# A four-layer graph network on one core: the last-but-one attention layer gathers normed rows and multiplies them by the weights tile by tile

## The reference, cut to what matters

```
h = jnp.maximum(_layernorm(x, axis=-1), 0.0)
x = x + _L2_gnn_ref(h, edge_index, L2_gnn_weight, L2_gnn_attn_l, L2_gnn_attn_r)

xt = jnp.matmul(x, weight).reshape(-1, heads, out_ch)      # heads 4, out_ch 64
row, col = (edge_index[0], edge_index[1])
alpha_l = jnp.einsum('ehd,hd->eh', xt[row], attn_l)
alpha_r = jnp.einsum('ehd,hd->eh', xt[col], attn_r)
alpha = jax.nn.softmax(jax.nn.leaky_relu(alpha_l + alpha_r, 0.01), axis=1)
tmp = jnp.einsum('nh,nhd->nd', alpha[:n], xt[col[:n]])
out = jnp.broadcast_to(tmp[:, None, :], (n, heads, out_ch))
```

## Time and profile before

| | us |
|---|---|
| median of 3 runs | 3559.73 |
| lowest, highest run | 3539.03, 3561.72 |
| the profiled execution, its time | 3567.03 |
| its span | 3565.2 |
| PE busy | 2424.9 (68%) |
| DVE busy | 2395.4 (67%) |
| POOL busy | 1734.6 (49%) |
| ACT busy | 1352.5 (38%) |

### The profile page before, as it was taken

How to read it: one execution, slowest core, us unless ns; L and a number is a source line. 1 busy time by engine, 2 the same in 40 slices (tenths; PEclk the granted TensorE clock), 3 DMA queues, 4 the chain that set the end, 5 groups by cost and what they waited for, 6 DMA issues and landing times. The chain is left out here.

```text
span 3565.2 us, 41686 instructions
## 1 busy us (share of the span) xinstructions
PE 2424.9 (68%) x12339; PEld 1976.6 (55%) x12339; DVE 2395.4 (67%) x4693; ACT 1352.5 (38%) x2800; POOL 1734.6 (49%) x1269
## 2 busy tenths in 40 slices
PE   4668733454555543666621999879999999925998
PEld 3522213454444443444421897469888988923788
DVE  5979945777777778877886544344565566615788
ACT  2268833444444441000000435424434434423776
POOL 0257887776667667888888777730000000042000
PEclk9779865555555555888855999889999999966999
DMA  9993224665555656555533774146545645340355
GB/s 373 351 355 34 22 26 130 174 171 164 165 165 166 172 170 137 133 142 134 143 40 39 202 177 89 1 103 185 175 126 172 185 130 173 118 103 8 109 173 176
DMA packets 338453, 517.84 MB, mean 145 GB/s; under 512 B 145379, under 2 KB 227100, under 8 KB 331580
## 3 DMA queue, kind: packets, MB, share of 16 engines
q1 hardware_dynamic: 190254, 436.41, 38.2%
q0 software_dynamic: 134768, 58.41, 14.2%
q10 hardware_dynamic: 13214, 20.35, 1.7%
HBM read 369.65 MB, written 145.38 MB: 144 GB/s over the span
## 5 line engine op out<-in xcount | busy, mean ns | idle before, releaser
L1133 PE MATMUL banks<-rows_r,lhs_r 128*128 128x448 f32 x3500 | 899.1, 372 | 84.0 <-issue 41.6
L728 POOL DMA_INDIRECT counts<-wts x391 | 637.4, 1630 | 307.9 <-DMA counts<-ring 141.0
L1133 PEld LDWEIGHTS banks<-rows_r,lhs_r 128*128 128x128 f32 x3500 | 667.8, 191 | 152.9 <-issue 74.8
L741 POOL DMA_INDIRECT weights<-wts x391 | 620.9, 1588 | 161.8 <-issue 159.1
L1133 PE MATMUL banks<-ring_r,lhs_r 128*128 128x448 f32 x1750 | 525.8, 370 | 0.0
L749 POOL DMA_INDIRECT reg<-tab_p,w x416 | 406.9, 978 | 217.9 <-issue 122.8
L548 DVE SCALAR_TENSOR_TENSOR ring_r<-ring,dinv,rows_r 128x896 fp32r<-128x896 f32 (+1 forms) x300 | 303.7, 1033 | 309.5 <-ACT rows_r L535 309.3
L1221 PE MATMUL banks<-lhs_r,oT 128*128 x416 | 203.3, 489 | 429.8 <-issue 346.6
L535 ACT ACTIVATE rows_r<-ring,dinv 128x896 fp32r<-128x896 f32 (+1 forms) x300 | 285.0, 951 | 399.3 <-PE banks L1133 342.0
L799 POOL DMA_INDIRECT el<-tab_l,base_i x25 | 24.0, 958 | 796.8 <-DMA tab_l<-reg 789.5
L1221 PEld LDWEIGHTS banks<-lhs_r,oT 128*128 128x128 f32 x416 | 131.9, 317 | 447.3 <-issue 447.0
(11 more groups left out here) (269 smaller groups left out, 4104.6 us busy)
## 6 DMA issues: line engine op xcount, KB each, us to landing
ring<-weights SPq DMA_DIRECT2D x225, 448.0 KB
ring<-counts SPq DMA_DIRECT2D x150, 448.0 KB
zbuf<-reg SPq DMA_DIRECT2D x208, 256.0 KB
reg<-zbuf SPq DMA_DIRECT2D x52, 1024.0 KB
counts<-ring SPq DMA_DIRECT2D x25, 1568.0 KB, 16.4
weights<-ring SPq DMA_DIRECT2D x25, 1568.0 KB
ring<-weights SPq DMA_DIRECT2D x75, 224.0 KB
dr<-low_rows_d SPq DMA_DIRECT2D x52, 256.0 KB
```

Source lines behind the costliest of these rows:

```text
L728: pool.indirect_dma_start(counts, bass.IndirectOffsetOnAxis(ap=ix_c[:, k:k + 1], axis=0), vals_c[:, k:k + 1], None, compute_op=ALU.add).th ...
L741: pool.indirect_dma_start(weights, bass.IndirectOffsetOnAxis(ap=ix_w[:, k:k + 1], axis=0), vals_w[:, k:k + 1], None, compute_op=ALU.add).t ...
L1133: m = pe.matmul(bank[:, 0:BLK], lhs[part], rows[:, c:c + BLK], start=first, stop=last)
```

## The change

Four things are changed.

1. The table `tab_x` holds the normed rows themselves (256 columns of `g_nat`) and no longer their product. SP stores a step as soon as ACT has written it.
2. PE no longer multiplies all 25 node tiles by 264 columns. It transposes them (`gT2`), and then makes only the left logits, 4 columns for each tile, all in one bank (stage `lg`); ACT copies them with one instruction and SP stores `tab_l`.
3. POOL issues the gathers of rows for steps 0 and 1 first, then waits for `tab_l`, and then alternates: left logits of step s-1, rows of step s+1.
4. When the rows of a step have landed, PE transposes each gathered tile (stage `gx`), ACT copies it to one of two buffers `edge_T`, PE multiplies it by 260 columns (stage `xt`), and ACT copies the product to `xt_edge`. ACT does these ten copies (`copy_rows(q)`) ahead of the exponential of the step, and `logits(q)` on DVE waits for the last of them.

The core of the diff:

```
+def rows_step(q):
+    ts = range(q * LG, (q + 1) * LG)
+    order = [(ts[0], "gx")]
+    for t in ts[1:]:
+        order += [(t, "gx"), (t - 1, "xt")]
+    return order + [(ts[-1], "xt")]
+
+def normed_groups(q):
+    return range(max(0, q - 2) * LG // 4 if q > 1 else 0, -(-NT // 4) if q == NSPLIT else max(0, q - 1) * LG // 4)
...
     # SP
             for s in range(NSPLIT):
-                sp.wait_ge(drained_a, nth[number["xt", ((s + 1) * LG - 1,)]])
-                if s == NSPLIT - 1:
-                    sp.dma_start(tab_l.rearrange("(t p) c -> p t c", p=P), xt_nat[:, :, XE:XW]).then_inc(l_stored, 16)
+                sp.wait_ge(ln_out, 2 * NT + (s + 1) * LG)
                 sp.dma_start(tab_x[s * LG * P:(s + 1) * LG * P].rearrange("(t p) c -> p t c", p=P),
-                             xt_nat[:, s * LG:(s + 1) * LG, 0:XE]).then_inc(xt_stored, 16)
+                             g_nat[:, s * LG:(s + 1) * LG, :]).then_inc(xt_stored, 16)
+            sp.wait_ge(drained_a, nth[number["lg", (0,)]])
+            sp.dma_start(tab_l.rearrange("(t p) c -> p t c", p=P), lg_nat).then_inc(l_stored, 16)
...
     # POOL
-            pool.wait_ge(l_stored, 16)
-            for s in range(NSPLIT):
-                for t in range(s * LG, (s + 1) * LG):
+            pool.wait_ge(xt_stored, 16 * NSPLIT)
+            for s in range(NSPLIT + 1):
+                for t in range(s * LG, (s + 1) * LG) if s < NSPLIT else ():
+                    pool.indirect_dma_start(x_edge[:, t, :], None, tab_x, ...).then_inc(edge_x[s], 16)
+                if s == 1:
+                    pool.wait_ge(l_stored, 16)
+                for t in range((s - 1) * LG, s * LG) if s else ():
                     pool.indirect_dma_start(el[:, t, :], None, tab_l, ...)
-                if s == 0:
-                    pool.wait_ge(xt_stored, 16 * NSPLIT)
-                for t in range(s * LG, (s + 1) * LG):
-                    pool.indirect_dma_start(xt_edge[:, t, :], None, tab_x, ...)
...
     # ACT
-            def copy_rows(g):
-                for t in tiles_of((g,), 4):
-                    bank = empty_bank(act, number["xt", (t,)])
-                    emptied(act.activation(xt_nat[:, t, :], bank[:, 0:XW], ACT.Copy))
+            def copy_rows(q):
+                for t, stage in rows_step(q):
+                    bank = empty_bank(act, number[stage, (t,)])
+                    if stage == "gx":
+                        emptied(act.activation(edge_T[t % 2], bank[:, 0:H], ACT.Copy))
+                    else:
+                        emptied(act.activation(xt_edge[:, t, :], bank[:, 0:XE], ACT.Copy))
...
             def exponentials(q):
+                copy_rows(q)
                 act.wait_ge(exp_in, q + 1)
...
     # PE
-            to_T("gT2", g_nat, ln_out, 2 * NT, behind=row_group)
-            to_T("gT3", g_nat, ln_out, 3 * NT)
+            to_T("gT2", g_nat, ln_out, 2 * NT)
+            bank = open_bank(number["lg", (0,)])
+            pe.wait_ge(drained_a, nth[number["gT2", (JH - 1, 6)]])
+            for t in range(NT):
+                for k in range(JH):
+                    m = pe.matmul(bank[:, t * HEADS:(t + 1) * HEADS], gT2[:, k, t * P:(t + 1) * P], gatw[:, k, XE:XW], ...)
+            m.then_inc(filled, 1)
+            def edge_rows(q):
+                pe.wait_ge(edge_x[q], 16 * LG)
+                for t, stage in rows_step(q):
+                    ...
+                    if stage == "xt":
+                        pe.wait_ge(drained_a, nth[number["gx", (t,)]])
+                    for k in range(JH):
+                        if stage == "gx":
+                            m = pe.transpose(bank[:, k * P:(k + 1) * P], x_edge[:, t, k * P:(k + 1) * P], ident[:, :])
+                        else:
+                            m = pe.matmul(bank[:, 0:XE], edge_T[t % 2][:, k * P:(k + 1) * P], gatw[:, k, 0:XE], ...)
+            for q in range(NSPLIT + 1):
+                if q < NSPLIT:
+                    edge_rows(q)
+                to_T("gT3", g_nat, ln_out, 3 * NT, groups=normed_groups(q))
...
     # DVE, logits(q)
-                v.wait_ge(edge_x[q], 16 * LG)
+                v.wait_ge(drained_a, nth[number["xt", ((q + 1) * LG - 1,)]])
```

48 lines of the change are left out of this document (21 added, 27 removed).

## The result

| | before | after |
|---|---|---|
| median, us | 3558.68 | 3594.48 |
| lowest, highest of 4 runs | 3539.03, 3561.72 | 3591.11, 3600.09 |
| the profiled execution's span | 3565.2 | 3589.3 |
| stage, first product of the node products to the fourth layer's products | 170.8 | 203.4 |
| ahead of the stage | 3094.4 | 3082.5 |

What follows compares the result with a forecast made beforehand. The third layer's stage, up to the fourth layer's products, was taken as the bound. Step 4 later by 5.4 us plus 10 for late hand-overs made +15 on 3559.7, stated as 3574; range 3546 to 3594, 8 in 10.

Steps and rivals of the forecast that it cites:

- narrow products: On PE ahead of the logits' store: 100 passes of 4 columns take 10 us, between 9 and 18.
- late hand-overs: Delayed dependent instructions on DVE beside POOL's gathers, steps 0 to 2: 10 us added, between 0 and 24.
- step 0: DVE's first step in the third layer's stage: begins at 3162 us, 8 us sooner, held by the logits.
- T: Ten ACT copies and the products between them, on the path in four steps: 9.4 us each, break-even 8.1.
- tail: From the start of step 4 to the fourth layer's products: same instructions, unchanged at 22.7 us.
- first row gather: POOL's first gather of rows in the stage: near 3131.3 us, against 3159.59 before.
- T of 11.0: Copies and products of a step with PE at half clock throughout: 11.0 us, making the time 3581.
- lock between VectorE and GpSimd: Shared SBUF port: only two-input DVE instructions late, by one gather of 0.96 us; set aside for the trace rows.
- The sum: Whole kernel: +5.4 for the start of step 4 and +10 for hand-overs, +15 on the median 3559.7.
- C: Rival, DVE's steps 0 and 1: hand-overs late through all gathers, +24 in place of +10, 3589; chance 0.22.
- B: Rival, a small gain: PE bursts warm or nearly so, or no hand-over late, 3551; chance 0.28.
- Past 1% only with T = 11.0 too: Claim on the slower rival: it passes 3595 only if T is also 11.0, adding 6.4; slower by over 1%, 0.08.

Runs made afterwards that it cites:

- both: Changed kernel with each step's ten copies made one step ahead and the 4-column products made group by group between transposes: 3455.42 us, ratio 0.9993 to the kernel before.
- lg_one_tile: Changed kernel with the 4-column products, and ACT's copy of the logits, cut to one of the 25 node tiles: 3602.21 us.
- ring_late_before: Kernel before, with SP issuing the six ring loads only after the last gather has landed: ratio 0.9994 to the kernel before.

## Why the prediction was wrong, point by point

Two terms of the sum failed. The narrow products were put at 10 us and took 21.5, and the late hand-overs were put at 10 us and took 25.7; the first moved the start of step 0, the second stretched step 1. The fourfold T, the main mechanism of the forecast, was right. That the median falls only half a microsecond outside the range is luck in part, since two smaller terms, T and the tail, were off the other way by 7.9 us together.

The forecast's places are put on before's clock, so after's times have 11.84 us added (3094.35 - 3082.51).

**The first row gather: right.** Forecast 3131.3. POOL's first, its wait for the logits, and its last gather:

```profile
3119.21 1.03 POOL L814 DMA_INDIRECT reg<-tab_x,tot  x1 [769.76 <-DMA tab_x<-reg]
...
3148.72 0.95 POOL L819 DMA_INDIRECT el<-tab_l,base_i  x1 [17.10 <-DMA tab_l<-reg]
...
3198.05 0.95 POOL L819 DMA_INDIRECT el<-tab_l,base_i  x1 [0.30 <-issue]
```

3119.21 + 11.84 = 3131.05. The pitch of a gather is 1.26 us, forecast 1.29.

**The narrow products: wrong, 10 forecast, 21.5 measured**, and outside the bounds of 9 and 18. Two errors are in that term. The clock: I took full clock "as PE has been at full clock for 29 us", but in those 29 us its list held the wide products that the change removes. After:

```profile
3107.00:3112.00 5.00, 3.52 (x17) 2.50 (x16) 1.28 (x11) 5.00 (x12) 0.00 (x0) 0.71 0.39 131
3112.00:3118.00 6.00, 4.20 (x15) 2.60 (x14) 0.00 (x0) 6.00 (x14) 0.00 (x0) 0.50 0.64 218
3118.00:3140.00 22.00, 21.51 (x101) 21.54 (x102) 0.00 (x0) 0.35 (x4) 9.68 (x10) 0.50 0.43 60
```

PE had only transposes beside layer norm 2, waited between them, and stood at half clock when the 50 products began, and through all of them. The price: I scaled by a row of 50 columns, 0.18 us at half clock, as an upper bound. The passes took 0.215, and PEld is busy for 21.54 of the 22 us. The 0.18 was misread: the start of the first of four pipelined products is not a full pitch ahead of the second. The weight loads of the same four products, in the trace before, are evenly spaced:

```profile
601.52 0.97 PEld L1230 LDWEIGHTS banks<-ring,reg 128*128 128x128 f32 x4
602.37 0.33 PEld L1221 LDWEIGHTS banks<-lhs_r,oT 128*128 128x128 f32 x1
```

They are (602.37 - 601.52) / 4 = 0.21 us apart. So 50 columns and 4 columns have the same pitch at half clock, which is that of the load of 128 weight columns ahead of each pass, and 100 passes at 0.21 would have given the 21.5 us. The Trainium skill, TensorE: Matmul & The Clock Gate, "LDWEIGHTS (loading the stationary operand)", gives the load's time by the stationary columns alone, as columns / 1.2, from which I estimate 107 ns for 128. The 0.12 us at full clock in the kernel *both* is near that. At half clock the measured 0.21 is twice as long, which the section does not say, and the measurement decides.

**Step 0: wrong, 3162 forecast, 3159.60 + 11.84 = 3171.4 measured**, 9.4 later. Nearly all of it is the term above. The products began at 3118.49 + 11.84 = 3130.3, close to the 3131 of the forecast, and POOL's first logit gather came at 3160.6 where the forecast had 3150.3, so 10.3 later; from there to step 0 it was 0.8 less than forecast. (That lg_one_tile puts step 0 at 3094.35 + 67.6 = 3162.0, as forecast, is a coincidence: its products take 1 us and not 10, and a late copy holds step 0.) So the mechanism, early rows gain nothing and the logits hold step 0, was right, and the size was off.

**T: nearly right, 9.4 forecast.** From step 0 to step 4 there are 107.3 us after. Without the 25.7 of hold-ups that is 81.6, and with the forecast's own terms (9.3 + 12.3 + 13.3 + 13.3 = 48.2) T = 8.4. On kind B, with no hold-up to take off, (81.2 - 48.2) / 4 = 8.3. The clock in the burst of step 4 is as forecast, half and then full:

```profile
3256.00:3262.00 6.00, 2.36 (x7) 1.90 (x8) 0.00 (x0) 4.01 (x10) 0.00 (x0) 0.50 0.00 0
3262.00:3267.00 5.00, 5.00 (x28) 4.25 (x28) 0.06 (x1) 2.76 (x9) 0.00 (x0) 0.93 0.00 0
```

The forecast had 7 us at half clock; here the clock is back to full for most of the second stretch (0.93). Four T gave 4.2 us less than the sum had. The rule of the Trainium skill that the forecast names (TensorE: Matmul & The Clock Gate, "Loop structure matters more than you think") is borne out in its direction, a product that waits for a copy finds the array cold; but T of 11.0, cold throughout, did not come. The rule fits better where I had not applied it, at the narrow products.

**The late hand-overs: right in kind, wrong in size and engine, 10 forecast, 25.7 measured.** I reasoned that they fell on DVE's step 0 and took half of a range of 0 to 24. They fell on ACT's copies in step 1, where PE and ACT hand over twenty times, and none was in step 0. The before trace had more to say than I read: its waits view lays 196 us of idle time on two engines to the same releaser, all of it between 570 and 1330 us, where POOL issues indirect DMAs (engine, what waited, us in all, times, longest):

```profile
DVE reg L1599 <- remote: 105.5, 28, 11.0
...
ACT reg L929 <- remote: 90.7, 32, 10.6
```

So it was there to be seen that ACT is hit as well as DVE, and by 10 us at a time. The forecast's upper end of 24 was the better estimate: the work on the path stood still for about 22 us before and 25.7 after, on another engine. The step down from 24 to 10 had no row behind it but the one undisturbed step of before. For the lock between VectorE and GpSimd, which the forecast weighed and set aside (the Trainium skill, SBUF — State Buffer, "SBUF: two separate sides"), the runs now say more. The section also names VectorE instructions in a two-port mode, which the forecast left out, but by its words ScalarE is not a party to the lock in either case. The late instructions after the change are ACT's, and their waits last up to 10.12 us against a gather's 0.96 on POOL.

**The tail: 22.7 forecast as unchanged, 18.9 measured.** Step 4 of before waits 4.39 us for the exponential, and in the sum for the steps I had already said that this is over, since ACT is free when the logits are ready. In the tail I forgot it: after, the wait is 0.65 us. The sum was inconsistent by 3.7 us.

**The sum.** Forecast for the start of the fourth layer's products: 3265.1 + 5.4 + 10 = 3280.5. Measured 3285.89 + 11.84 = 3297.7, 17.2 later: +9.4 (products) - 4.2 (four T) + 15.7 (hold-ups) - 3.7 (tail). To the median's +35.8 against +15 another 3.6 us are missing. The part behind the stage was 3.3 longer in the two traces (298.5 to 307.0 in all runs, and as long in ring_late_before as in the changed kernel), and I put no cause to it.

**The rivals.** C, late hand-overs through all gathers at 3589, was the nearest. Its size is what happened (24 against 25.7), on another engine and in another step than it said; T and the products decided the rest. B fell with the narrow products and the hold-ups. "Past 1% only with T = 11.0 too" was wrong because no rival carried the price of the products: the upper bound of 18 us was computed and then left out of every case. With it (+8) C gives 3597.

## What to carry to other kernels

When a change takes work away from an engine whose clock depends on being busy, price what comes behind it at half clock; and price a stream of narrow matrix products by the load of its weights, not by its width. Work that moves from ahead of a round trip through memory to behind it has to be put where the engines that wait for it have something else to do: here the ten copies cost 8 us a step in front of the exponential, and nearly nothing one step ahead. And a wait that the trace lays to no engine of the program is worth a look over the whole launch: if it comes only beside one kind of transfer, it can hit whatever stands beside that transfer after the change, on more than one engine.

## What the runs showed of the hardware

- On chips of kind A, ACT's and DVE's instructions with their inputs ready start up to 11 us late in some stretches where POOL's indirect DMAs are in flight. The waits laid to "remote" came to about 160 to 240 us over a launch (DVE and ACT together, not all on the path); on two chips of kind B the traces show none. The kernel before takes 3556 to 3571 us on the one and 3456 to 3461 on the other, and reaches its third layer's stage at 3094 and 3007 us: the same program differs by 3% from chip to chip, which is more than the change is worth.
- Some lengths of these waits recur. Of the 48 in ACT's copies of the stage, in all traces of kind A, 23 were 3.12, 4.52, 5.21, 6.61, 8.70, 9.41 or 10.11 us, which differ by multiples of 0.7 us. I know no cause for that, nor for the point at which they start.
- A pass of an fp32 product with 128 weight columns and 4 moving columns costs 0.21 us at half clock and 0.12 at full; at half clock the weight loads of passes with 50 moving columns have the same pitch, 0.21.
- A store of 3200 pieces of 16 bytes took 8.2 us to land in both kernels, and a gather of 128 rows costs POOL 1.26 us, the same for rows of 16 and of 1024 bytes.
